# One DMA in place of four per probability tile, with query rows left in another order in the fetched tile

## The reference

```python
qg = q.reshape(b, HKV, G, s, HD)                     # 8 key/value heads, G = 4 query heads each, HD = 128
scores = jnp.einsum('bkgqd,bksd->bkgqs', qg, k) / math.sqrt(HD)
bias = jnp.where(rel > 0, NEG_INF, slopes[:, :, None, None] * rel)
attn = jax.nn.softmax(scores + bias[None], axis=-1)
out = jnp.einsum('bkgqs,bksd->bkgqd', attn, v)
```

## Time and profile before

| | us |
|---|---|
| median of 3 runs (2056.29 to 2061.45) | 2059.68 |
| the profiled execution's own time | 2058.6 |
| its span, first to last instruction | 2056.5 |
| PE busy in the span | 1993.2 |
| DVE, POOL, ACT busy | 1363.5, 1189.2, 1162.6 |

### The profile page before, as it was taken

The page is one execution under the profiler, slowest core; times in us unless marked ns, Lnnn a source line. Parts: engine busy times, 40 slices in busy tenths (PEclk is TensorE's granted clock), DMA queues, the critical chain, the costliest instruction groups (busy, mean ns, idle before and its releaser), DMA issues.

```text
span 2056.5 us, 33589 instructions
## 1 busy us (share of the span) xinstructions
PE 1993.2 (97%) x10956; PEld 1698.1 (83%) x10956; DVE 1363.5 (66%) x3431; ACT 1162.6 (57%) x3314; POOL 1189.2 (58%) x1188
## 2 busy tenths in 40 slices
PE   7999999999999999999999899999999999999996
PEld 6888888888888888888888788787878878788774
DVE  6667667666666666768876566565666656566696
ACT  4656656565665656655555465555656555465552
POOL 3574645647465574655645557465664746657473
PEclk9999999999999999999999999999999999999998
DMA  4573855657466573765635637365463745637254
GB/s 164 138 161 119 192 141 150 132 154 166 129 171 145 136 159 113 181 181 142 135 109 141 142 96 173 96 154 139 123 124 108 172 101 137 161 81 165 69 122 99
DMA packets 896141, 283.81 MB, mean 138 GB/s; under 512 B 677721, under 2 KB 839513, under 8 KB 895969
## 3 DMA queue, kind: packets, MB, share of 16 engines
q1 hardware_dynamic: 844064, 179.44, 41.7%
q10 hardware_dynamic: 51904, 102.24, 14.2%
HBM read 152.59 MB, written 128.97 MB: 137 GB/s over the span
## 4 chain that ended last, share of the span: by engine, by line
PE 76%; SPq 8%; DMA 4%; DVE 4%; issue 4%; POOL 2%; ACT 2%; DVEq 0%; POOLq 0%; ACTq 0%
PE s_ps L1106 16%; PE q_ps L1106 15%; PE y_ps L1106 14%; PE o_ps L1106 14%; PE turn_ps L1193 9%; SPq L653 7%; PE turn_ps L1106 7%; DMA p_bounce<-probs_odd 2%; POOL probs_odd L881 1%; DMA p_raw_b<-p_bounce 1%; DMA p_bounce<-probs_even 1%; DVE oT_lo L1029 1%; PE turn_ps L1187 1%; SPq L642 1%; ACT oT_hi L823 1%
## 5 line engine op out<-in xcount | busy, mean ns | idle before, releaser
L881 POOL TENSOR_TENSOR probs_odd<-probs_odd,p_inv 128x256 f32<-128x256 f32 (+3 forms) x256 | 318.0, 1257 | 180.1 <-DVE p_inv L1008 179.2
L881 POOL TENSOR_TENSOR probs_even<-probs_even,p_inv 128x128 f32<-128x128 f32 (+3 forms) x256 | 261.3, 1043 | 191.3 <-DVE p_inv L1008 190.5
L1106 PE MATMUL s_ps<-kT_hi,qT_hi 128*128 128x512 f32 (+3 forms) x768 | 272.5, 355 | 4.1 <-DVE neg_max L1001 3.8
L1001 DVE CUSTOM_DVE_ANT_0 probs_odd<-s_ps,rel 128x256 f32<-128x256 f32 (+3 forms) x256 | 209.3, 820 | 97.3 <-issue 96.6
L802 ACT ACTIVATE probs_odd<-probs_odd,neg_max 128x256 f32<-128x256 f32 (+3 forms) x256 | 212.2, 831 | 91.7 <-DVE neg_max L1001 91.6
L1106 PE MATMUL s_ps<-kT_hi,qT_lo 128*128 128x512 f32 (+3 forms) x768 | 262.4, 342 | 0.0
L1106 PE MATMUL s_ps<-kT_lo,qT_hi 128*128 128x512 f32 (+3 forms) x768 | 261.7, 341 | 0.0
L802 ACT ACTIVATE probs_even<-probs_even,neg_max 128x128 f32<-128x128 f32 (+3 forms) x256 | 185.1, 725 | 118.7 <-DVE neg_max L1001 118.4
L1001 DVE CUSTOM_DVE_ANT_0 probs_even<-s_ps,rel 128x128 f32<-128x128 f32 (+3 forms) x256 | 174.9, 687 | 109.8 <-issue 108.8
L987 DVE STREAM_TRANSPOSE p_raw<-p_raw 128x512 f32<-128x512 f32 x252 | 174.9, 700 | 83.5 <-DMA p_raw<-p_bounce 83.2
L1106 PE MATMUL q_ps<-wqT_hi,xnT_hi 128*128 128x512 f32 x512 | 217.2, 424 | 1.0 <-DVE qn L1012 0.8
(11 more groups left out here) (131 smaller groups left out, 5068.3 us busy)
## 6 DMA issues: line engine op xcount, KB each, us to landing
p_raw<-p_bounce SPq DMA_DIRECT2D x1008, 64.0 KB, 2.3
p_bounce<-probs_odd SPq DMA_DIRECT2D x60, 384.0 KB, 3.1
p_raw_b<-p_bounce SPq DMA_DIRECT2D x256, 64.0 KB, 2.4
p_bounce<-probs_odd SPq DMA_DIRECT2D x60, 256.0 KB, 2.8
p_bounce<-probs_even SPq DMA_DIRECT2D x60, 256.0 KB, 3.0
p_bounce<-probs_even SPq DMA_DIRECT2D x64, 192.0 KB, 2.4
wq_kept<-wqT_hi ACTq DMA_DIRECT2D x8, 1024.0 KB, 4.5
wq_kept<-wqT_lo ACTq DMA_DIRECT2D x8, 1024.0 KB, 6.8
```

The source lines that it names most:

```text
L881: nc.gpsimd.tensor_tensor(row, row, p_inv[:, s % 2, h:h + 1].to_broadcast((P, L)), ALU.mult).then_inc(sems["normalise"], 1)
L1001: nc.vector.tensor_tensor_reduce(out=probs[s % 2][:, h, 0:L], in0=s_ps[:, at_col:at_col + L], in1=rel[:, S - L:S], scale=-float(slopes[w % ...
L1106: last = nc.tensor.matmul(target, a, m, start=start and i == 0 and k == 0, stop=stop and i == len(pairs) - 1 and k == 2)
```

## The change

The fetch becomes one DMA of 128 partitions. For this, `p_bounce` is laid out by head, key tile, block of 32 keys, query and key in the block, so that a send writes runs of 32 numbers (128 bytes) where it wrote runs of 128 numbers (512 bytes); a fetch reads, for each partition and head, four neighbouring queries by 32 keys (512 bytes in a run) where it read 128 bytes at a time. After the transpose of 32x32 blocks, a partition of the raw tile has the queries in the order 0, 4, 8, ..., 1, 5, 9, ...; `upper_p` and `lower_p` read it with a step of 32 numbers (128 bytes) from one element to the next, and write in order.

```diff
+        def rows_in_order(tile):
+            return tile.rearrange("p (h a i) -> p h i a", h=G, a=NBLK)
+
+        def by_row(tile):
+            return tile.rearrange("p (h i a) -> p h i a", h=G, a=NBLK)
...
-        p_bounce = nc.dram_tensor("p_bounce", [2, NT, G, P, P], F32).ap()
+        p_bounce = nc.dram_tensor("p_bounce", [2, G, NT, NBLK, P, BLOCK], F32).ap()
...
-                sp.dma_start(p_bounce[s % 2, first:s + 1, h].rearrange("u p c -> p u c"),
-                             probs[s % 2][:, h, first * P:(s + 1) * P].rearrange("p (u c) -> p u c", c=P)).then_inc(p_sent[s % 2], 16)
+                sp.dma_start(p_bounce[s % 2, h, first:s + 1].rearrange("u b p j -> p (u b) j"),
+                             probs[s % 2][:, h, first * P:(s + 1) * P].rearrange("p (u j) -> p u j", j=BLOCK)).then_inc(p_sent[s % 2], 16)
...
-                blocks = p_bounce[s % 2, j].rearrange("h (a i) (b j) -> b i (h a) j", i=BLOCK, j=BLOCK)
-                for b in range(NBLK):
-                    sp.dma_start(raw_p(n)[b * BLOCK:(b + 1) * BLOCK, :].rearrange("p (n j) -> p n j", j=BLOCK),
-                                 blocks[b]).then_inc(p_fetched[n], 16)
+                tile = p_bounce[s % 2, :, j].rearrange("h b (i a) j -> (b i) h (a j)", a=NBLK)
+                sp.dma_start(raw_p(n).rearrange("p (h k) -> p h k", h=G), tile).then_inc(p_fetched[n], 16)
...
-                nc.scalar.activation(p_high(p_slot[w, s, j]), raw_p(raw_tile[w, s, j]), ACT.Copy).then_inc(sems["upper_p"], 1)
+                nc.scalar.activation(by_row(p_high(p_slot[w, s, j])), rows_in_order(raw_p(raw_tile[w, s, j])), ACT.Copy).then_inc(sems["upper_p"], 1)
...
-                nc.gpsimd.tensor_tensor(p_low(r), raw_p(raw_tile[w, s, j]), p_high(r).bitcast(F32), ALU.subtract).then_inc(sems["lower_p"], 1)
+                nc.gpsimd.tensor_tensor(by_row(p_low(r)), rows_in_order(raw_p(raw_tile[w, s, j])), by_row(p_high(r).bitcast(F32)), ALU.subtract).then_inc(sems["lower_p"], 1)
...
-                dve.wait_ge(p_fetched[raw_tile[w, s, j]], 16 * NBLK * raw_uses[w, s, j])
+                dve.wait_ge(p_fetched[raw_tile[w, s, j]], 16 * raw_uses[w, s, j])
```

## The result

| | us |
|---|---|
| changed kernel, median of 7 runs (2062.86 to 2068.36) | 2064.48 |
| kernel before, 7 runs beside them (2054.45 to 2061.45) | 2057.57 |
| ratio, with its 95% interval | 1.0037 [1.0027, 1.0047] |
| span of the profiled execution, before and after | 2056.5, 2066.3 |

The changed kernel is slower by some 7 us, where 4 us faster was forecast. It lies inside the range that was given (2041 to 2105), and inside the likeliest case's own (2046 to 2067), but on the other side of no change.

What follows compares the result with a forecast made beforehand. PE, busy 97% of the span, was taken as the bound, with SP's fetch issues showing at second-batch group ends; -8 us gained there and +4 given back made -4, so 2059.7 became 2055.7, say 2056, range 2041 to 2105.

Steps and rivals of the forecast that it cites:

- likeliest case: Moderate read price, with SP's pace at group ends replaced by POOL's: own range 2046 to 2067, chance 0.40.
- SP's issues, packets, landings: 948 of 1264 fetch DMAs go; a tile needs 0.5 us of SP, not 2.1, and lands after 2.8 us.
- The prices of the reads: `upper_p` and `lower_p`, reading with a step, each take 0.40 us longer: 0.63 to 1.03 and 1.30 to 1.70.
- The second batch: Its eight groups gain 8 us at their ends, less 0.25 us a group for longer reads.
- the eight gains of 1.0: In each of the second batch's eight groups, block 7's last `lower_p` ends 1.0 us sooner.
- the formula: Block 7's end in group 10: 1412.8 + 10x, x the added read price; 1416.8 at 0.40, against 1417.84 before.
- What is given back: In all 16 groups, longer reads on POOL and ACT cost 0.25 us a group, between 0 and 1: +4 us.
- Cheap reads: Rival: the step costs ACT and POOL nothing, and block 7 ends at about 1412.4: 2042 us, chance 0.18.
- Dear small writes: Rival: in block 7's sends, 128-byte packets to DRAM cost more; 2077 us at 16 ns, above 2140 at 27.7; chance 0.14.
- Dear reads: Rival: at block 7's six `lower_p` POOL becomes the bound from x = 0.5; 2088 us at 0.8, chance 0.28.
- the signs that were to show the prediction wrong: `lower_p` above 1.9 or below 1.4, send packets above 15 ns, or PE's `qn` or direct-tile waits above 8 us.

Runs made afterwards that it cites:

- e10: The changed kernel with the stepped reads only in groups 8 to 15, plain reads in groups 0 to 7 (rows out of order there): 2050.4 us.
- e1: The changed kernel with plain reads of the raw tile on both ACT and POOL, rows of memory tiles left out of order: 2038.4 us.
- e5: The kernel before with each head sent in 128-byte runs, still four fetches a tile and plain reads: 2163.4 us.
- e12: e1 with the rows put back where `o_high` and `o_low` read PSUM with a 128-byte step, direct tiles turned with a reordered identity: 2038.4 us.
- e14: e12 with the scratch tile laid out for fetches in 2-KB runs, direct tiles reordered by their copies from PSUM: 2034.4 us, 0.9896 of the kernel before.
- e13: The changed kernel with plain reads of the raw tile, rows put back by PE reading the `values` moving operand with a 128-byte step: 2070.5 us.

## Why the prediction was wrong

- **SP's issues, packets, landings: right.** The fetch issues fell from 643 to 191 us. 128-byte packets took 13.9 ns and 512-byte ones 28.9 in the mean (12.7 and 28.2 before, worked out over the whole trace), so small writes to DRAM carry next to no penalty of their own. The fetch landed after 3.3, 2.8 forecast, the 384 KB send after 5.0, 4 to 5.5 forecast.
- **The prices of the reads: off by a third, one up, one down.** 0.40 was taken for both; ACT's is 0.54, POOL's 0.29. No row of before had a step on either engine. The Trainium skill (GPSIMD Engine Reference, Performance pitfalls for Q7 kernels) gives half as much again for such reads; the estimate from it was 0.56 us, and the trace shows half of that, with one of two inputs stepped.
- **The second batch: right in sum, in part by luck.** e10 has plain reads in the first batch, where its groups are as long as before, and the whole change in the second. Its median is 6.2 us under the kernel before, where the forecast for that batch was -8 + 8 x 0.25 = -6. But the eight gains of 1.0 are not there: six groups gained 1.1 each on average, group 8 lost 0.5 and group 15 1.9. And in group 10, which the formula was built on, 0.4 of the 1.0 us came, with POOL's idle 1.46 us and the cheaper tiles as errors against each other.
- **The step that failed is "What is given back", in the first batch.** It said: "Slack takes most of it: PE has next to no waits there now. Between 0 and 1 us a group, I take 0.25: 16 x 0.25 = +4." For the first batch that is +2 of the 4. Measured are +14.1 us there (the medians of the changed kernel and e10; +13.6 by the groups of the two traces), with 3.6 to 5.1 in groups 0 and 7 each, against a bound of 1. That alone turns a forecast of -4 into a loss. The step asked who stands behind a longer `upper_p` or `lower_p` on its engine. It didn't ask what those two hold: with three raw tiles in the first batch, a tile's fetch waits for the `lower_p` three tiles back, so what the two take longer can be paid again in each turn of the ring. The chain of group 0 shows one such turn, from 150.72 to 161.41. "No waits of PE now" said that there was slack, not how much.
- **The clock** wasn't in the sum. A 1.8 us wait of PE was followed by 3.4 us at half the clock, which adds some 1.7 us. It falls three times in the changed kernel's trace before the last 14 us and not at all in that of before, some 5 us together; this execution's mean granted clock is 0.994, that of the fastest of the seven 0.998, so in others it seems to fall less.
- **The rivals.** "Cheap reads" gave 2042 for reads that cost nothing; e1 measured 2038.4. "Dear small writes" looked at the packet's price and found it harmless, rightly (13.9 ns); what e5 shows is that small sends are dear by another way, with longer issues of SP, more packets and waiting flips, and that the new fetch pays for it. "Dear reads" had the right mechanism, and even named the three raw tiles of the first batch, but only from a price of 0.5 us on POOL and behind the six `lower_p` of block 7: at 0.54 and 0.29 us the first batch already lost 14 us. All the signs that were to show the prediction wrong stayed quiet (`lower_p` 1.59, send packets 13.9 ns, 6.2 us of waits for `qn`, no longer than before), since none looked at memory tiles of the first batch.

Not settled: how much of the 14 us is the ring, how much flips and `normalise` that stand behind a longer neighbour, and how much the clock. That the ring is the main part is argued from one turn of it; no run had a fourth raw tile in the first batch.

## What to carry to other kernels

Before a stage that isn't on the path is made longer, measure its slack: take, tile by tile, the time between its end and its user's start, and look at what it holds (buffers in a ring) as well as at what queues behind it. A reordering that has to be paid somewhere belongs where the data is read from PSUM: there it was free on ACT and DVE, while the same step on an SBUF read cost 0.54 us on ACT, 0.29 on POOL and 0.04 on PE for 512 elements. And a transfer's two ends have to be changed and priced together: small sends with the old fetches cost 106 us here, and the new fetch gave 125 back; the sum hides both.

## What the runs showed of the hardware

- ACT on SBUF, 512 fp32 a partition: 628 ns plain, 1172 with a 128-byte step on the read, 1141 with a 16-byte step on the write. The Trainium skill (SBUF — State Buffer, Specifications (TRN2)) says that SBUF's lines have 16 bytes and want at least two hits each for full bandwidth; by that rule both steps miss alike, and the trace agrees for ACT (0.54 and 0.51 us).
- ACT and DVE on PSUM: 596 against 597 and 686 against 685 ns with a 128-byte step on the read (e12), 596 against 597 and 677 against 677 with a 16-byte step (e14). The Trainium skill (Advanced Engine Details and Errata, PSUM Cachelines) wants every two elements of PSUM contiguous for full rate in matmuls; for these two engines' reads no run here shows any such price.
- PE's moving operand from SBUF with a 128-byte step: 436 and 458 ns against 395 and 419 (e13).
- An issue of SP costs 0.36 us at the median for a fetch of 512 runs and 0.50 for a send of 3072. It takes longer where many packets of the queue haven't ended: all 37 issues at 3000 or more took over 1 us in the changed kernel, all 73 in e5, the longest 7.0 us.
